# A graph layer on one core: 18 unread matmuls on TensorE ahead of the first layer's node blocks

## The reference

```
x = layernorm(x + L0(x))     # attention over edges, 4 heads of 16, then a dense step
x = layernorm(x + L1(x))     # mean of the neighbours

L0: ZU = Z @ U               # (N, 4 heads x 16)
    alpha = softmax over the edges of each dst of (zs * zd).sum / 4
    agg = segment_sum(alpha * zs)
    Z_half = 0.5 Z + 0.5 * sum_k w_k agg_k @ U_k.T
    out = relu(Z_half + 0.5 * (Z_half - Z_half Dmat.T Dmat) @ Dmat - 0.05)
L1: out = relu(mean_agg @ W_l.T + b_l + x @ W_r.T) + x
```

## Time and profile before

| | us |
|---|---|
| median of 3 runs | 4599.48 |
| the 3 runs | 4597.17, 4599.48, 4620.62 |
| the profiled execution | 4618.69 |
| its span, first to last instruction | 4616.9 |

### The profile page before, as it was taken

The page is one execution under the profiler, slowest core; times in us unless marked ns, Lnnn a source line. Parts: engine busy times, 40 slices in busy tenths (PEclk is TensorE's granted clock), DMA queues, the critical chain, the costliest instruction groups (busy, mean ns, idle before and its releaser), DMA issues. The chain is left out here.

```text
span 4616.9 us, 27468 instructions
## 1 busy us (share of the span) xinstructions
PE 930.4 (20%) x3111; PEld 610.2 (13%) x3111; DVE 2277.8 (49%) x9483; ACT 778.7 (17%) x1408; POOL 3353.7 (73%) x3541
## 2 busy tenths in 40 slices
PE   7301101112111000000094211222222221112037
PEld 7201001001001000000042100111111110001025
DVE  2107665665665565566563443443344344334447
ACT  2001001001001000000043222222222222222225
POOL 6677777777777777777565777777777777777765
PEclk6556555555556555555586555555555555555569
DMA  9713333333333222222275666666665666666579
GB/s 350 303 37 120 120 93 94 120 93 94 120 104 96 84 88 77 79 88 88 74 248 192 219 215 236 231 209 215 236 231 206 234 229 207 235 236 213 197 244 316
DMA packets 329803, 793.61 MB, mean 172 GB/s; under 512 B 78246, under 2 KB 216843, under 8 KB 300228
## 3 DMA queue, kind: packets, MB, share of 16 engines
q1 hardware_dynamic: 149906, 378.14, 23.0%
q0 software_dynamic: 139488, 279.69, 20.4%
q10 hardware_dynamic: 40274, 134.62, 7.4%
HBM read 420.40 MB, written 371.83 MB: 172 GB/s over the span
## 5 line engine op out<-in xcount | busy, mean ns | idle before, releaser
L473 POOL DMA_INDIRECT sb_big<-x,sb_idx x1564 | 1481.3, 947 | 513.0 <-issue 476.4
L473 POOL DMA_INDIRECT sb_big<-zu_rows,sb_idx x1564 | 1479.4, 946 | 490.4 <-issue 476.1
L1300 DVE SCALAR_TENSOR_TENSOR ps_V<-ps_V,sb_keepc,sb_big 128x256 f32<-128x256 f32 x1518 | 747.8, 493 | 132.5 <-ACT sb_big L901 79.3
L901 ACT COPY sb_big<-ps_V 128x1024 f32<-128x1024 f32 (+1 forms) x414 | 399.7, 966 | 1309.6 <-DVE ps_V L1300 1306.4
L654 PE MATMUL ps_T<-sb_ident,sb_xg 128*128 128x128 f32 x392 | 114.2, 389 | 2445.3 <-DMA sb_xg<-x 1232.4
L1300 DVE SCALAR_TENSOR_TENSOR ps_V<-ps_E,sb_keepc,sb_big 128x256 f32<-128x256 f32 x46 | 22.7, 492 | 1041.8 <-DMA sb_big<-x,sb_idx 1002.2
L1067 DVE TENSOR_TENSOR sb_big<-ps_V,sb_big 128x2176 f32<-128x2176 f32 x46 | 111.5, 2424 | 591.9 <-DMA sb_big<-zu_rows,sb_idx 591.9
L654 PEld LDWEIGHTS ps_T<-sb_ident,sb_xg 128*128 128x128 f32 x392 | 71.6, 200 | 2502.9 <-issue 1738.1
L1061 DVE TENSOR_TENSOR_SCAN ps_V<-ps_V,sb_big 128x34 f32<-128x34 f32 x2944 | 356.9, 208 | 17.4 <-issue 17.4
L1110 DVE TENSOR_TENSOR_SCAN sb_big<-ps_E,sb_big 128x34 f32<-128x34 f32 x2944 | 355.3, 203 | 1.6
L473 POOL DMA_INDIRECT sb_hn<-rows,sb_nidx x196 | 191.4, 976 | 87.6 <-issue 54.9
(11 more groups left out here) (229 smaller groups left out, 1732.5 us busy)
## 6 DMA issues: line engine op xcount, KB each, us to landing
rows<-sb_big SPq DMA_DIRECT2D x46, 3072.0 KB, 10.6
rows<-sb_big SPq DMA_DIRECT2D x46, 1280.0 KB, 10.5
rows<-sb_big ACTq DMA_DIRECT2D x46, 1224.0 KB, 5.4
z_at_start<-sb_big ACTq DMA_DIRECT2D x46, 1088.0 KB, 8.5
sb_big<-z_at_start SPq DMA_DIRECT2D x46, 1088.0 KB
sb_xg<-in_x_dram SPq DMA_DIRECT2D x42, 768.0 KB
own<-sb_hn SPq DMA_DIRECT2D x28, 896.0 KB, 11.5
sb_big<-own SPq DMA_DIRECT2D x28, 896.0 KB
```

Source lines behind the costliest of these rows:

```text
L473: pool.indirect_dma_start(to, None, table, bass.IndirectOffsetOnAxis(ap=index.bitcast(U32), axis=0), **more).then_inc(done, 16)
L901: act.copy(slot1[s][:, cols, :], V0[:, first_word:first_word + width].rearrange("p (c f) -> p c f", f=D)).then_inc(col_copied, 1)
L1300: dve.scalar_tensor_tensor(out=sums_at(j), in0=before, scalar=keepc[:, j:j + 1], in1=slot1[s][:, j, :], op0=ALU.mult, op1=ALU.add).then_in ...
```

## The change

`dense(0)` is preceded by a new function, `warm_up(18)`. It waits for the last of `background(0)`'s results to have left PSUM (it writes the bank `O[0]`, which `background(0)` used) and for `mend_dma` to reach 32, and then issues 18 matmuls: a 128 x 128 piece of `M` is the stationary operand, all of `M`, 128 x 512, the moving one. Each starts a new sum, so nothing accumulates, and `dense(0)` overwrites the bank later. No other engine's program is changed, and no semaphore is raised by the new matmuls.

```
@@ block.tensor
                 rounds(pe, NG // 2, body)
 
+            def warm_up(n):
+                pe.wait_ge(bg_out[0], GB * NG)
+                pe.wait_ge(mend_dma, 32)
+                for k in range(n):
+                    pe.matmul(O[0], M[:, 0, 0:P], M[:, :, :].rearrange("p k n -> p (k n)"), start=True, stop=True)
+
+            warm_up(18)
             dense(0)
             background(1)
```

## The result

The changed kernel takes 4597.25 us (median of 23 runs, 4590.6 to 4617.67). The kernel before, run as often beside it, takes 4622.07 (4594.47 to 4651.04): the three runs that stood at 4599.48 are among these 23 and were a low draw, two of them the second and the third lowest. The ratio of after to before is 0.9958, 95% interval 0.994 to 0.9977. The record doesn't say how it is formed; the quotient of the two medians, 0.9946, lies in the interval. The change makes the kernel faster by about 0.4 to 0.5%, and it makes the runs alike. But for one run of 4617.67, which is the profiled one, all of after's lie between 4590.6 and 4606.43, while before's fill 57 us.

What follows compares the result with a forecast made beforehand. TensorE bounds layer 0's node blocks, partly at half clock. 16.8 us gained less 2.1 us delay gives 14.7 for the profiled execution (4604.0); low runs change +0.6, so the predicted median is 4600, range 4586 to 4611.

Steps and rivals of the forecast that it cites:

- The new stretch: TensorE's time in `dense(0)` with the clock up from the first transpose: 14 groups of 9.70 us, 135.8 instead of 152.6.
- The rise: TensorE's clock going from 1.2 to 2.4 GHz during the new matmuls, taken as 4.6 us after their start.
- The transfers fit: In `dense(0)`, 113.0 us of DMA work would fit the new stage's 137.9 us, a share of 0.82, without delaying TensorE.
- B: Clock rises in the new matmuls but falls back in `dense(0)`; 2.1 us added, median 4601.6; chance 0.05.
- C: New matmuls stay at 1.2 GHz, ending 15.2 us late, and `dense(0)` opens slowly: 4633.9 us; chance 0.05.
- the opening of another group: In `dense(0)`, the clock may rise at a different group's start in each execution, costing 7.7 us per later group.
- How that stands to the median: Step from the profiled execution to before's three runs: low ones gain nothing (+0.6 us), giving a median of 4600.1.
- 1.5 us to give: Loss in `dense(0)` of a run whose clock is up 3.4 us after TensorE's start; the change costs it 2.1.
- My own formula: In `dense(0)`, slow time before the clock's rise costs 0.443 of itself: 1.5, 9.2 or 17.0 us for successive openings.
- the 23 us that I took for the limit: Whole-kernel difference, about 0.5%, needed to tell a change: faster below 4576.5 us, slower above 4622.5.
- what comes from elsewhere: Difference between the low runs and the profiled execution not explained by `dense(0)`'s slow opening, put at 4 to 6 us.
- Rival A: Low runs have the slow opening of `dense(0)` too, so every run gains 14.7 us: median 4584.8; chance 0.13.

Runs made afterwards that it cites:

- before_b: The kernel before the change, unedited, second of three further profiles: 4599.18 us, the clock rising 21.0 us after TensorE's start in `dense(0)`.
- the paired form: Changed kernel with 18 calls, plus one 512-column identity matmul per pair of blocks in `dense(0)` instead of two of 256: 4597.42 us.
- the other paired profile: Kernel before, without the new matmuls, with one 512-column identity matmul per two blocks in `dense(0)`: median 4593.44 us, profiled execution 4587.87 us.

## Why the prediction was wrong

*Right.* TensorE bounds the node blocks and its end sets layer 1's start. The new stretch was put at 135.8 us and is 135.8. From the start of the new matmuls to the end of layer 0 it was put at 153.6 and is 152.9 (2294.34 to 2447.21). The new matmuls were put at 17.8 us and took 17.1 to 18.4. The rise was put at 4.6 us and came between 3 and 6. The transfers fit. Rivals B and C did not come about. That the rise can fall on the opening of another group, at 7.7 us more for each, was right as well: four executions gave 21.0, 38.4, 73.3 and 90.8 us. The Trainium skill's rule that the number of slow matmuls at a start changes from run to run (page "TensorE: Matmul & The Clock Gate", section "What's actually happening") agrees with these four. In size they go beyond the 6 to 14 of its example: in the first profile alone 82 instructions were slow.

*Wrong.* I forecast no change, and the interval of the ratio leaves out 1. The 4597.25 itself is near the 4600 forecast; what was wrong is what before takes without the change. The step that failed is "How that stands to the median": I took the two low runs "as executions whose clock rose at once", and by the median of three made them the kernel, so that its typical run had "1.5 us to give". Over 23 runs before's median is 4622.07, and the two low runs are the second and third lowest. My own formula, 0.443 of the time to the rise, and the 21 to 91 us of the four profiles give losses of 9.3 to 40.2 us, 24.8 in the mean.

The change pays 1.5 to 2.8 of that (from the mend's store to the first transpose it takes 19.5 to 20.8 us in three profiles, 18.0 before). Had I put a draw of openings into the forecast of before, and not the three runs, the four profiles would have given a gain of some 7 to 38 us, in two of them by more than the 23 us that I took for the limit; the medians differ by 24.8. That limit was mis-sized too: the interval of the ratio is 0.2% to either side, not 0.5%.

Whether the two low runs rose at once can't be told, since neither was profiled. It can be so: the executions with 32 rows (4598.34) and with 6 calls (4598.37) came to `dense(0)` with a low clock and rose 3.1 and 3.6 us after its start. It can be otherwise: before_b took 4599.18 with a loss of 9.3 us and a rest 11.8 us shorter than the profiled execution's (4454.3 against 4466.1). Of these 11.8 us, 7.3 lie ahead of the mend's store (2276.50 against 2283.80), nearly all in POOL's wait for the projection (7.1 us against 13.9). I had put what comes from elsewhere at 4 to 6 us; the first profile's rest was the longest of four, and I had no second one to see that by.

*Rival A* did not come about as stated. Its 4584.8 is 12 us under the measured median, and none of the 23 runs comes below 4590.6. But before_b shows a low run with a slow opening, only a shorter one than A has.

## What to carry to other kernels

Where a stage's speed hangs on something that is drawn anew in each run, work out the stage's time as a function of the draw, and forecast both kernels from that, not from a median of three. Compare the stage in two profiles, not the spans. Unread matmuls that bring TensorE to its full clock were worth while here, where it is the bound right after. They had to run nearly up to the first real instruction: the clock was lost after a gap of 2.02 us in one profile and held over 0.97 us in another. And 18 calls too many cost 18.8 us.

## What the runs showed of the hardware that was not expected

Matmuls 32 rows high ran for 15.6 us without raising the clock; 128 rows high, it rose in 3 to 6 us. `dense(0)`, half of whose matmuls are 64 rows high, took 21.0 to 90.8 us of unbroken work to raise it in four profiles of the kernel before, each time in a group's opening, where the transposes stand; with 32 rows and with 6 calls it took 3.1 and 3.6 us in one profile each, in the first opening. What in the opening raises it wasn't tested. Once up it held through the same work. In the paired form it fell inside the stage twice, in waits of 2.46 and 2.05 us; in the other paired profile, with waits of at most 1.69 us, it held.
